# Feed-forward rows 4 to 7: the normalized x turned by VectorE in 32x32 blocks and through HBM, where TensorE turned it

## The reference, cut to what matters

```
x = x + 0.5 * ffn(layernorm(x))
x = x + mamba(layernorm(x))
x = x + 0.5 * ffn(layernorm(x))

ffn(x):                       # x: tokens x 128
  scores  = sigmoid(x @ router_w.T)                     # 16 experts
  s       = scores + bias
  groups  = 4 groups of 4 experts; group score = sum of its two best s; keep the 2 best groups
  picked  = the 4 best experts of s in the kept groups
  combine = 2.5 * scores[picked] / sum(scores[picked]), 0 elsewhere
  y       = sum over e of combine[:, e] * (silu(x @ gate[e]) * (x @ up[e])) @ down[e]
  return y + (silu(x @ sh_gate) * (x @ sh_up)) @ sh_down   # 2 shared experts
```

## Time and profile before

| | us |
|---|---|
| median of 3 runs | 922.81 (922.42 to 925.47) |
| profiled execution, its own time | 924.45 |
| its span, first to last instruction | 922.7 |
| PE busy in the span | 882.2 (96%) |
| DVE busy | 738.9 (80%) |
| POOL busy | 663.8 (72%) |
| ACT busy | 569.3 (62%) |
| PE busy from 140 to 178 us (rows 3:0 to 3:17 of f1) | 38.00 of 38.00 |
| PE busy from 598 to 918 us (f2) | 315.05 of 320.00 |
| granted TensorE clock, share of full speed | 0.991 over the span, 1.00 in both feed-forward layers |

### The profile page before, as it was taken

The page is one execution under the profiler, slowest core; times in us unless marked ns, Lnnn a source line. Parts: engine busy times, 40 slices in busy tenths (PEclk is TensorE's granted clock), DMA queues, the critical chain, the costliest instruction groups (busy, mean ns, idle before and its releaser), DMA issues. The chain is left out here.

```text
span 922.7 us, 12303 instructions
## 1 busy us (share of the span) xinstructions
PE 882.2 (96%) x3599; PEld 626.6 (68%) x3599; DVE 738.9 (80%) x1248; ACT 569.3 (62%) x1008; POOL 663.8 (72%) x485
## 2 busy tenths in 40 slices
PE   8899999999999999999999887889999999999997
PEld 7677778787767765455445433467878778778885
DVE  5969869777974578999999999966977887696664
ACT  6465575565564778888977593236557556555553
POOL 7658666676756566999999886646667677676765
PEclk9999999999999999999999989899999999999999
DMA  7633454343433333434444334244434545345440
GB/s 202 199 124 103 127 148 116 119 138 102 132 97 106 95 95 110 144 128 162 142 160 137 117 137 125 82 140 126 117 123 111 150 135 144 110 113 159 152 126 23
DMA packets 102547, 117.14 MB, mean 127 GB/s; under 512 B 37960, under 2 KB 61648, under 8 KB 102480
## 3 DMA queue, kind: packets, MB, share of 16 engines
q1 hardware_dynamic: 102480, 116.36, 41.7%
HBM read 109.77 MB, written 6.55 MB: 126 GB/s over the span
## 5 line engine op out<-in xcount | busy, mean ns | idle before, releaser
L681 POOL TENSOR_TENSOR act_lo<-act,act_hi 128x512 fp32r<-128x512 f32 x288 | 374.8, 1304 | 211.9 <-ACT act_hi L774 211.5
L767 ACT ACTIVATE bank<-bank 128x512 f32<-128x512 f32 x252 | 146.6, 582 | 232.7 <-PE bank L1067 225.7
L977 DVE TENSOR_TENSOR sg<-bank,c_ring 128x512 f32<-128x512 f32 x252 | 172.0, 683 | 95.2 <-ACT bank L767 93.0
L1063 PE MATMUL bank<-x_parts,w_hi 128*128 128x512 f32 x572 | 235.0, 411 | 8.8 <-DVE act L955 6.2
L955 DVE SCALAR_TENSOR_TENSOR act<-sg,bank 128x512 f32<-128x512 f32 x288 | 197.9, 687 | 45.3 <-PE bank L1067 30.2
L1067 PE MATMUL bank<-x_parts,w_hi 128*128 128x512 f32 x572 | 225.7, 395 | 0.0
L1064 PE MATMUL bank<-x_parts,w_lo 128*128 128x512 f32 x572 | 225.6, 394 | 0.0
L774 ACT ACTIVATE act_hi<-act 128x512 fp32r<-128x512 f32 x288 | 179.4, 624 | 1.2 <-PE bank L1047 0.8
L1063 PEld LDWEIGHTS bank<-x_parts,w_hi 128*128 128x128 f32 x572 | 107.6, 188 | 45.8 <-DVE act L955 15.3
L1064 PEld LDWEIGHTS bank<-x_parts,w_lo 128*128 128x128 f32 x572 | 107.8, 188 | 25.2 <-issue 2.6
L1067 PEld LDWEIGHTS bank<-x_parts,w_hi 128*128 128x128 f32 x572 | 107.6, 188 | 25.4
(11 more groups left out here) (184 smaller groups left out, 1048.1 us busy)
## 6 DMA issues: line engine op xcount, KB each, us to landing
c_ring<-c_dram SPq DMA_DIRECT2D x252, 256.0 KB, 3.5
c_ring<-c_dram SPq DMA_DIRECT2D x64, 512.0 KB, 3.7
y_dram<-out_t SPq DMA_DIRECT2D x56, 64.0 KB, 2.8
y_tok<-y_dram SPq DMA_DIRECT2D x14, 256.0 KB, 3.7
out<-x_sb SPq DMA_DIRECT2D x8, 256.0 KB, 2.4
x_sb<-in_L_attn_hidden_states SPq DMA_DIRECT2D x3, 512.0 KB, 6.0
stage<-in_L_ffn_gate_w SPq DMA_DIRECT2D x4, 256.0 KB, 4.8
stage<-in_L_ffn_up_w SPq DMA_DIRECT2D x4, 256.0 KB, 4.9
```

The source lines that it names most:

```text
L681: self.nc.gpsimd.tensor_tensor(m["act_lo"][:, g % LAG], m["act"][:, g % ACTS], m["act_hi"][:, g % LAG].bitcast(FP32), ALU.subtract).then_i ...
L767: nc.scalar.activation(self.s_bank[:, g % 2], self.h_bank[:, g % 2], ACT.Silu).then_inc(self.sg_ready, 1)
L977: nc.vector.tensor_tensor(m["sg"][:, g % 2], silu, weight, ALU.mult).then_inc(self.w_done, 1)
L1063: nc.tensor.matmul(dst, m["w_hi"][:, k, n, :], x_hi, start=True, stop=False)
```

## The change

For rows 4 to 7 of both feed-forward layers:

- PE's transposes of `xn` and ACT's copies out of PSUM are gone. DVE turns `xn` (SBUF) in 32x32 blocks into `out_t` (SBUF), one instruction a row, at steps 8 and 12.
- SP stores `out_t` to a new HBM tensor `xt_dram` in four DMAs of 64 KB with pieces of 128 bytes, which puts the blocks in place, and loads the row back to `xt` in one DMA of 256 KB. `out_t` is shared with the turned sums, so both uses wait for each other's stores.
- Logits are at step 18, scores at 19, the 14 routing pieces at steps 20 to 33.
- Step 0 lies two blocks earlier: at 35 (1:17) and 71 (3:17). So statistics, `shift` and normalizing come two blocks earlier, logits, scores and every routing piece three blocks later.

Rows 0 to 3 keep their way, and so does the Mamba layer.

```diff
+FAR_ROW = 4
+        xt_dram = nc.dram_tensor("xt_dram", (2, BATCH, D, SEQ), FP32, kind="Internal").ap()
...
+FAR = Prep((6, 7), (8, 12), (), 18, 19, {20 + n: 1 for n in range(14)})
...
-    PAIRED = {2: 6, 4: 37, 6: 73}, {2: 1, 4: 37, 6: 73}
+    XT_STORED = 16 * P // Q
+    PAIRED = {2: 6, 4: 35, 6: 71}, {2: 1, 4: 35, 6: 71}
...
+    def prep_of(self, r):
+        return FAR if r and r >= FAR_ROW else SLOW
...
+        def store_xt(r):
+            sp.wait_ge(self.norm.xt_ready, self.first + r + 1)
+            for a in range(P // Q):
+                sp.dma_start(xt[r].rearrange("(b k) (t q) -> k t b q", k=Q, q=P)[:, :, :, a * Q:(a + 1) * Q],
+                             m["out_t"][a * Q:(a + 1) * Q].rearrange("k (t b q) -> k t b q", t=TT, q=Q)
+                             ).then_inc(self.xt_stored, 16)
+        def load_xt(r):
+            sp.wait_ge(self.xt_stored, self.XT_STORED * (r - FAR_ROW + 1))
+            sp.wait_ge(self.x_lo_ready, r - 1)
+            sp.dma_start(m["xt"][:, r % 2], xt[r]).then_inc(self.xt_loaded, 16)
+        far = {13: (store_xt, 0), 15: (load_xt, 0), 17: (store_xt, 1), 19: (load_xt, 1)}
...
+                w = r * E + e - (FAR_ROW - 2) * E
+                if w >= 0 and w // E < BATCH - FAR_ROW and w % (2 * E) in far:
+                    move, n = far[w % (2 * E)]
+                    move(FAR_ROW + 2 * (w // (2 * E)) + n)
...
+    def dve_turn_xn(self, dve, r):
+        m = self.m
+        dve.wait_ge(self.norm.xn_ready, self.first + r + 1)
+        dve.wait_ge(self.y_stored, 16 * D // Q * (r // 2 * 2 - 2))
+        need(dve, self.xt_stored, self.XT_STORED * (r - FAR_ROW))
+        self.nc.vector.transpose(m["out_t"][:, :], m["xn"][:, r % 2].rearrange("p t d -> p (t d)")
+                                 ).then_inc(self.norm.xt_ready, 1)
+
     def dve_turn_out(self, dve, i):
         dve.wait_ge(self.down_done, (i + 1) * NE)
+        if i >= FAR_ROW - 2:
+            dve.wait_ge(self.xt_stored, self.XT_STORED * min(i // 2 * 2 - FAR_ROW + 4, BATCH - FAR_ROW))
...
+                    if at is FAR and step in at.turn:
+                        self.dve_turn_xn(dve, r + at.turn.index(step))
-                    if step == min(SLOW.route):
+                    if step == min(at.route):
...
-        pe.wait_ge(self.xt_copied, r + rows)
+        for n in range(rows):
+            self.wait_xt(pe, r + n)      # xt_copied below row 4, xt_loaded from row 4 on
...
-                if step in SLOW.turn:
-                    self.pe_transpose_xn(pe, r + SLOW.turn.index(step))
-                if step == SLOW.logits:
+                at = self.prep_of(r)
+                if at is SLOW and step in at.turn:
+                    self.pe_transpose_xn(pe, r + at.turn.index(step))
+                if step == at.logits:
```

More of the change, by code:

```diff
@@ L559, in __init__ @@
         self.y_stored, self.y_loaded = sem("y_stored"), sem("y_loaded")
+        self.xt_stored, self.xt_loaded = sem("xt_stored"), sem("xt_loaded")
         self.xt_copied, self.logits_ready, self.tanh_ready, self.score_ready = (
@@ L596, in load_weights_of_rows @@
         m = self.m
-        y = m["y_dram"][self.p]
+        y, xt = m["y_dram"][self.p], m["xt_dram"][self.p]
         rows = None if self.out is None else self.out.rearrange("b (t p) d -> b p t d", p=P)
@@ L699, in act_copy_xt, with wait_xt @@
         nc.scalar.activation(m["xt"][:, r % 2], self.misc, ACT.Copy).then_inc(self.xt_copied, 1)
+    def wait_xt(self, eng, r):
+        if r < FAR_ROW:
+            eng.wait_ge(self.xt_copied, r + 1)
+        else:
+            eng.wait_ge(self.xt_loaded, 16 * (r - FAR_ROW + 1))
     def act_high_x(self, ae, r):
         nc, m = self.nc, self.m
-        ae.wait_ge(self.xt_copied, r + 1)
+        self.wait_xt(ae, r)
         nc.scalar.activation(m["x_hi"][:, r % 2], m["xt"][:, r % 2], ACT.Copy).then_inc(self.x_hi_ready, 1)
@@ L780, in act_blocks @@
                 r, step = self.step_of(g)
[L781 to L785, removed]
+                at = self.prep_of(r)
+                if step in at.apply:
+                    norm.act_apply(ae, self.first + r + at.apply.index(step))
+                if step in at.copy:
+                    self.act_copy_xt(ae, r + at.copy.index(step))
+                if step == at.scores:
                     self.act_scores(ae, r, 2)
@@ L994, in dve_blocks @@
                 if step is not None:
-                    if step == min(SLOW.route):
+                    at = self.prep_of(r)
+                    if at is FAR and step in at.turn:
+                        self.dve_turn_xn(dve, r + at.turn.index(step))
+                    if step == min(at.route):
                         routing = self.dve_route(dve, r, 2)
-                    for _ in range(SLOW.route.get(step, 0)):
+                    for _ in range(at.route.get(step, 0)):
                         next(routing)
```

## The result

| | before | after |
|---|---|---|
| median (range), us | 923.19 (922.42 to 925.47, 4 runs) | 939.03 (937.65 to 940.57, 4 runs) |
| span of the profiled execution, us | 922.7 | 938.8 |
| granted TensorE clock over the span | 0.991 | 0.984 |

The ratio after to before is 1.0165, 95% interval 1.0147 to 1.0184. The forecast had the sign and +3.9 us; the time lies beyond its range and beyond every rival.

What follows compares the result with a forecast made beforehand. PE was taken to set the pace nearly everywhere. The sum -3.5 + 5.25 + 2.2 = +3.9 us gave 926.7 us on the median of 922.81; the range for 8 in 10 was 920.6 to 928.8 us.

Steps and rivals of the forecast that it cites:

- The DMAs: SP's stores and loads of turned rows: the second row's end two blocks before the logits, so they cost 0.
- The third rival: Ring loads run 4 us longer beside 128-byte pieces: 1 to 3 us more at four row starts, 931 us; chance 0.06.
- What PE gains: PE in the feed-forward layers: 8 sets of transposes go at 0.44 us each, a gain of 3.5 us.
- The turn on DVE: DVE's eight turns, 0.70 us each, keep lateness below 1.9 us, so they cost PE 0.
- The moved routing: DVE's routing pieces, held by POOL, make PE wait: 5.25 us over three pairs, 2.2 more at f1's end.
- What will show it: Trace signs; first ones: product behind removed transposes follows at 0.23, L853 of rows 4 and 6 over 1.2 us, not 0.29.
- the prediction's own rule: Small elementwise DVE instructions starting during POOL's 128x512 operation are held until it ends; those reading PSUM are not.
- Only PE's gain: L853 starts 0.15 us earlier, ahead of POOL's operation, and lateness decays: -3.9, 918.9 us; chance 0.15.
- Half of it: The cascade of held DVE instructions begins but L876 or L892 escapes: 0.1 in all, 922.9 us; chance 0.17.
- the forecast's stall pattern: PE's waits per pair behind held DVE instructions; 0.4 us lighter or heavier a pair gives 925.3 to 928.3 us.

Runs made afterwards that it cites:

- e1: On the changed kernel, SP in f2 stores each finished output row one row later, so no wait for POOL's add just before the x store: 929.07 us.
- e6: On e1, SP in f1 also waits for POOL's add of the row before, with no store behind it: 933.44 us, ratio 1.0102.
- e9: On e1, f2's output store is back at its old place, but of a row added long before: 928.89 us, ratio 1.0052.
- e10: On e6, a 256 KB store to an unused HBM tensor is put behind f1's wait: 939.59 us, ratio 1.0163.
- e5: Kernel before the change without TensorE's transposes of rows 4 to 7, ACT's copies kept: 920.57 us, ratio 0.9962.
- e4: Changed kernel with TensorE's transposes and ACT's copies for rows 4 to 7 again, at the new steps, no HBM trip: 932.90 us, ratio 1.0097.
- e3: On e1, L853 (L888 after the change) of rows 4 to 7 is issued at the head of routing piece 3: 919.10 us, ratio 0.9944.
- e2: On e1, the 14 routing pieces of rows 4 to 7 begin at step 19, not 20: 919.37 us, ratio 0.995.

## Why the prediction was wrong, step by step

**The DMAs (0 us taken; 11.2 us in fact).** This step failed: "The second row's store and load, 5 and some 4 us, end two blocks before the logits, six blocks (12.5 us) behind its turn ... I take 0". It counted the margin from when the data is ready. The margin runs from when SP gets there: 4.7 us later in f2 (712.63 to 717.33). From there to PE's start at 727.66 it took 10.3 us, where the prediction had 5 and some 4: the last of the four stores landed at 722.70, the load went out at 722.72 and landed 4.81 later. PE was ready at 723.89, 11.26 us behind the end of the turn: 4.70 + 10.33 - 11.26 is the wait of 3.77 us. Without the 4.7 us the row would have been there 1 us before PE, less than the two blocks of the prediction, but in time. I named what stands *behind* SP's waits and did not ask what SP waits for *ahead* of the store. The third rival looked at this queue as well, but at the ring; the ring never ran dry (no engine of the changed kernel waits for a ring load). e1, e6, e9 and e10 show the cause from four sides: without the wait 929.1, with the store but no standing wait 928.9, with the wait alone in f1 933.4, with both in f1 939.6.

**The clock (not in the sum).** Of the 11.2 us the two waits are 6.7 (3.77 and 2.96). Nearly all of the other 4.4 us is PE at the lower level after it had stood: 3.1 (1.40 + 1.92 less 0.21) and 0.5 in the blocks behind, the rest in the logits' own blocks. The Trainium skill has this in "TensorE: Matmul & The Clock Gate", "Part 1": two levels, 1.2 and 2.4 GHz, the lower one behind an idle stretch. The trace agrees at both waits, 0.50 and 0.53 granted.

**What PE gains (-3.5).** Right: -3.5 by e5.

**The turn on DVE (0).** Right: eight instructions of 0.70 us, none of them held by POOL, although each began 0.73 to 0.75 us into a POOL instruction of 1.3 us. The blocks around them have no excess in PE. From the list of that line in the changed kernel:

```profile
L976 DVE STREAM_TRANSPOSE out_t<-xn x8: 703/704/706, 120.1 to 795.6; 128x512 f32<-128x512 f32 x8
```

**The moved routing (+5.25 and +2.2).** The mechanism was right, the size some 1.5 us low (9.0 by e4; 8.6 by PE's excess in the blocks of the four pairs). DVE of the changed kernel in row 3 of f2:

```profile
740.52 1.29 DVE L888 TENSOR_TENSOR g_ge<-g_ge,g_gt 128x128 f32<-128x128 f32 x1
...
743.37 0.42 DVE L893 TENSOR_SCALAR g_in<-g_rank 128x32 f32<-128x32 f32 x1
...
745.02 0.99 DVE L897 TENSOR_TENSOR masked<-biased,g_in 128x128 f32<-128x128 f32 x1
...
751.52 1.38 DVE L911 TENSOR_TENSOR tied<-masked,top 128x128 f32<-128x128 f32 x1
...
759.35 1.27 DVE L927 TENSOR_TENSOR picked<-picked,score 128x128 f32<-128x128 f32 x1
```

L888 is the old L853, 0.29 in the earlier trace rows: held, as the first sign of "What will show it" asked, and the instructions named after it are held in turn. In e1, whose f2 has no other disturbance, PE's excess in a pair is 0.14, 0.32, 0.28, 0.42 and 1.01, 2.17 in all, where the working had 0.03, 0.31, 0.21, 0.14 and 1.18, 1.87. The other pairs show the same within 0.1. For f1's last pair the working had 3.96, 2.2 more than before; blocks 96 to 108 show 4.8 (2.46, 0.79 and 0.64 the largest) against 2.4 before, 2.4 more. That PE would lose over 3 us there came true; the wait of 1 us in 3:14 as well. DVE's lateness in 3:2 to 3:6 of f2 was 0.58, 1.19, 1.94, 1.81 and 2.27, where the working had 0.55, 1.17, 1.94, 1.83 and 2.24. That it would stay at 1.9 or more up to 3:14 did not hold throughout: it was 1.66 and 1.18 in 3:7 and 3:8, then 2.05 to 3.23 from 3:9 to 3:14.

One reading in this part of the prediction was wrong. The 0.30 of the earlier trace rows is not the free time of the held L892: that row reads and writes `bank`, which is PSUM, and by the prediction's own rule such an instruction is never held. The conclusion stands, since e3 has the SBUF one in a free place:

```profile
745.07 0.29 DVE L932 TENSOR_TENSOR picked<-picked,score 128x128 f32<-128x128 f32 x1
```

**The rivals.** *Only PE's gain* priced what e2 and e3 do: -3.9 forecast, -4.6 and -4.8 measured. The mechanism behind it, a start of L853 outside the hold, was right; in the change itself it did not happen. *Half of it* did not either. The range failed because it held no case for a store of x late in its queue: its upper end was the forecast's stall pattern a bit heavier, and e1's +5.1 us would have lain within it. So the sign of the forecast was earned by its mechanism, but that mechanism is only a third of the measured time.

## What to carry to other kernels

When a DMA is put into a queue that issues in order, list every wait ahead of it at its new place, in each phase of the program that runs this code, and count its margin from when the queue gets there. A long wait in a DMA queue that costs nothing today is a trap for whatever is put behind it. Where VectorE is near its limit beside GpSimd, as here, look at the phase at which a small VectorE instruction starts before its length: one of 0.3 us, moved in four places, gave 10 us in all.

## What the runs showed of the hardware

- **A DVE instruction held by POOL waits for the instruction, not for the stream.** A 0.29 us TENSOR_TENSOR took 1.27 against one POOL instruction of 512 columns and 0.71 when it was cut in two. A TENSOR_SCALAR with one SBUF input was held as well: L893 above, 0.42, and 0.18 as L898 in e3. The Trainium skill, "SBUF — State Buffer", section "SBUF: two separate sides", names two SBUF inputs or a two-port mode as what takes the lock; whether this instruction runs in such a mode no run here shows. The SBUF to SBUF transpose never was held (703 to 706 ns eight times, each begun while POOL ran).
- **What PE's standing does to its clock.** A wait of 1.03 us was followed by no fall (e6). Waits of 2.75 to 3.8 us were each followed by 0.50 to 0.54 over the next 3.5 us (the changed kernel, e10). Near 2 us the same pause goes either way: 2.04 us in e6 was followed by 0.62, and the wait before block 104 of f1 by 1.00 in the changed kernel (2.17 us) but by 0.61 in e9 (2.21 us):

```profile
251.20:254.70 3.50, 2.96 (x12) 2.12 (x13) 3.36 (x15) 1.71 (x3) 2.64 (x3) 1.00 0.00 0
```
```profile
251.10:254.60 3.50, 3.50 (x10) 2.78 (x11) 3.36 (x15) 0.58 (x1) 2.69 (x3) 0.61 0.00 0
```

- **Four stores of 64 KB in pieces of 128 bytes** cost SP 2.6 us of issuing and landed after 2.7 us (median; the old ones of `y_dram` 2.8). The load of 256 KB behind them landed after 4.0 us in the median, and after 4.81 and 4.25 in the two late places; the other six took 3.1 to 4.5, so no run here shows that lateness itself makes it slower.
